# Split A-item epilogues and two-slot sigmoid buffers in an eight-core gated block

## What is computed

```python
xn = _layernorm(x, axis=-1)

# branch 1 (D_MODEL 2048, D_INNER 4096)
xn2 = (xn - mu) * rsqrt(var + 1e-5) * gamma + beta
z, gate = split(einsum('bsd,ed->bse', xn2, W_in), 2, axis=-1)
z_gated = z * sigmoid(clip(z, -15.0, 15.0))
z_temporal = z_gated * softmax(-dt)
b1 = einsum('bse,de->bsd', z_temporal * silu(clip(gate, -15.0, 15.0)), W_out) + xn

# branch 2 (H 2048, I 8192; weights are (int - 128) * scale)
g = einsum('bsh,ih->bsi', xn, Wg)
u = einsum('bsh,ih->bsi', xn, Wu)
b2 = einsum('bsi,hi->bsh', silu(g) * u, Wd)

return x + b1 + b2
```

## Time and profile before

| | us |
|---|---|
| median of 2 runs | 9599.44 (9590.61 to 9608.28) |
| profiled execution, its own time | 9556.24 |
| its span, slowest core (core 0) | 9554.7 |
| spans of the eight cores | 9482.8 to 9554.7 |
| TensorE busy, core 0 | 8093.0 |
| VectorE busy, core 0 | 3246.1 |
| ScalarE busy, core 0 | 755.3 |
| GpSimd busy, core 0 | 1138.1 |

### The profile page before, as it was taken

How to read it: one execution, slowest core, us unless ns; L and a number is a source line. 1 busy time by engine, 2 the same in 40 slices (tenths; PEclk the granted TensorE clock), 3 DMA queues, 4 the chain that set the end, 5 groups by cost and what they waited for, 6 DMA issues and landing times.

```text
span 9554.7 us, 87681 instructions; the slowest of 8 cores (9482.8 to 9554.7 us)
## 1 busy us (share of the span) xinstructions
PE 8093.0 (85%) x36127; PEld 3627.5 (38%) x36864; DVE 3246.1 (34%) x3151; ACT 755.3 (8%) x684; POOL 1138.1 (12%) x1093
## 2 busy tenths in 40 slices
PE   0006999999995899999996799999997788999998
PEld 0002444444442344444442344444443333444443
DVE  5542223333342232333333223233334232333334
ACT  3220000000000000000000000000000000000000
POOL 1000001111110010111110000111110101111110
PEclk9998999999997999999998899999998899999999
DMA  5554568777775567878776566777777566777777
GB/s 186 186 148 48 67 67 97 75 78 76 77 99 90 64 69 91 77 74 79 74 79 123 56 68 89 74 75 78 76 77 137 51 70 69 87 80 73 79 74 127
DMA packets 2296440, 827.99 MB, mean 87 GB/s; under 512 B 1997025, under 2 KB 2259185, under 8 KB 2287857
## 3 DMA queue, kind: packets, MB, share of 16 engines
q0 software_dynamic: 1857056, 570.53, 58.1%
q1 hardware_dynamic: 285394, 151.13, 6.4%
q10 hardware_dynamic: 153600, 100.69, 4.3%
HBM read 1241.64 MB, written 83.90 MB: 139 GB/s over the span
## 4 chain that ended last, share of the span: by engine, by line
PE 72%; DMA 13%; DVE 2%; issue 2%; another core or an unknown queue 1%; ACTq 1%; DVEq 1%; ACT 0%; POOL 0%; POOLq 0%
PE psZ L626 16%; PE psG L626 16%; DMA w1r<-w_inT 9%; PE psZ L571 9%; PE psOa L654 8%; PE psG L571 8%; PE psOb L654 8%; DMA wdr<-wdT 2%; PE psOa L571 1%; DMA xtck<-x_dt 1%; PE psOa L597 1%; PE psOb L597 1%; ACTq L733 1%; PE psOb L571 1%
## 5 line engine op out<-in xcount | busy, mean ns | idle before, releaser
L571 PE MATMUL psZ<-xnslot,w1r 128*128 128x512 bf16 x3513 | 880.5, 411 | 1160.7 <-DVE xnslot L810 805.3
L626 PE MATMUL psZ<-xnslot,gur 128*128 128x512 bf16 x7527 | 1691.9, 380 | 21.5 <-DVE gur L794 10.5
L626 PE MATMUL psG<-xnslot,gur 128*128 128x512 bf16 x7529 | 1687.5, 379 | 8.0
L794 DVE TENSOR_SCALAR gur<-gur 128x2048 bf16<-128x2048 bf16 x512 | 355.6, 696 | 2553.3 <-DMA gur<-wgT 1641.9
L626 PEld LDWEIGHTS psZ<-xnslot,gur 128*128 128x128 bf16 x7680 | 752.1, 98 | 924.7 <-issue 23.2
L626 PEld LDWEIGHTS psG<-xnslot,gur 128*128 128x128 bf16 x7680 | 751.4, 98 | 906.2
L571 PEld LDWEIGHTS psZ<-xnslot,w1r 128*128 128x128 bf16 x3584 | 365.6, 104 | 1674.9 <-issue 1337.0
L714 POOL DMA_DIRECT2D gur<-wgT x256 | 293.8, 1148 | 4527.5 <-PE psG L626 4198.3
L571 PE MATMUL psG<-xnslot,w1r 128*128 128x512 bf16 x3513 | 790.4, 380 | 3.8
L829 DVE TENSOR_SCALAR zcb<-psZ 128x1024 bf16<-128x1024 f32 x112 | 137.1, 1224 | 1770.8 <-PE psG L571 1706.9
L757 ACT ACTIVATE szcb<-psZ,sb_sg 128x1024 bf16<-128x1024 f32 x240 | 267.4, 1114 | 4826.0 <-PE psZ L626 4549.9
(11 more groups left out here) (86 smaller groups left out, 5435.1 us busy)
## 6 DMA issues: line engine op xcount, KB each, us to landing
w1r<-w_inT POOLq DMA_DIRECT2D x256, 512.0 KB, 9.6
gur<-wgT POOLq DMA_DIRECT2D x256, 512.0 KB, 8.7
gur<-wuT POOLq DMA_DIRECT2D x256, 512.0 KB, 12.2
wdr<-wdT POOLq DMA_DIRECT2D x256, 512.0 KB, 13.6
w2r<-wo_bf SPq DMA_DIRECT2D x256, 256.0 KB, 7.8
gx<-x_td SPq DMA_DIRECT2D x32, 1024.0 KB, 25.7
wo_in<-w_outT POOLq DMA_DIRECT2D x32, 1024.0 KB, 8.5
xtck<-x_dt ACTq DMA_DIRECT2D x64, 512.0 KB, 5.0
```

Of the source, the lines that this page charges most:

```text
L571: e.matmul(ps[:, th * TH:(th + 1) * TH], w1r[:, sl * 2048 + dc * 128: sl * 2048 + (dc + 1) * 128], xnslot[:, dc * TILE + th * TH: dc * TIL ...
L626: e.matmul(ps[:, th * TH:(th + 1) * TH], gur[:, sl * 2048 + dc * 128: sl * 2048 + (dc + 1) * 128], xnslot[:, dc * TILE + th * TH: dc * TIL ...
L794: M.do(lambda e, buf=buf: e.tensor_scalar_add(buf, buf, -128.0), c_dv, ("guc", t, c) if nn % 2 == 1 else None)
```

## The change

`zcb`, `gcb`, `szcb` and `sgcb` get two slots each; item i uses slot i mod 2 (C items: c mod 2, `szcb` only). On ScalarE, the sigmoid of C item c waits for `h` of c-2 instead of c-1.

On VectorE the work on an A item is cut into two functions. `ep_s1(i)` holds the wait for the item and the two clamps; `ep_s2(i)` waits for the sigmoids and does the three products (events `zg` and `act`). Up to i = 8 the list position of A item i holds `ep_s1(i)` and then `ep_s2(i-1)`; from i = 9 it holds `ep_s2(i-1)` and then `ep_s1(i)`; the position of item 31 ends with `ep_s2(31)`. The evictions of B items keep their places in the list. New waits of VectorE on its own events are added: `act` of i-1 in `ep_s2`, `h` of c-1 (or `act` of 31) before the first operation of a C item. The number of operations and of DMAs is the same, and TensorE's code and its waits are not changed.

```diff
@@ -494,10 +494,10 @@
             w2r = sst.enter_context(nc.sbuf_tensor("w2r", [128, R_W2 * 1024], BF16))
             gur = sst.enter_context(nc.sbuf_tensor("gur", [128, R_GU * 2048], BF16))
             wdr = sst.enter_context(nc.sbuf_tensor("wdr", [128, R_WD * 2048], BF16))
-            zcb = sst.enter_context(nc.sbuf_tensor("zcb", [128, TILE], BF16))
-            gcb = sst.enter_context(nc.sbuf_tensor("gcb", [128, TILE], BF16))
-            szcb = sst.enter_context(nc.sbuf_tensor("szcb", [128, TILE], BF16))
-            sgcb = sst.enter_context(nc.sbuf_tensor("sgcb", [128, TILE], BF16))
+            zcb = sst.enter_context(nc.sbuf_tensor("zcb", [128, 2 * TILE], BF16))
+            gcb = sst.enter_context(nc.sbuf_tensor("gcb", [128, 2 * TILE], BF16))
+            szcb = sst.enter_context(nc.sbuf_tensor("szcb", [128, 2 * TILE], BF16))
+            sgcb = sst.enter_context(nc.sbuf_tensor("sgcb", [128, 2 * TILE], BF16))
             p1b = sst.enter_context(nc.sbuf_tensor("p1b", [128, TILE], BF16))
             p2b = sst.enter_context(nc.sbuf_tensor("p2b", [128, TILE], BF16))
             xtck = sst.enter_context(nc.sbuf_tensor("xtck", [128, 2 * TILE], F32))
@@ -739,23 +739,27 @@
                 xp_half(M, d_xp, "X2", x2_scr, 0, range(16))
                 for t in range(nt):
                     for i in range(32):
+                        sl = (i % 2) * TILE
                         M.wait(c_dv, ("zc", t, i))
-                        M.do(lambda e: e.activation(szcb[:, :], zcb[:, :],
-                                                    AF.Sigmoid),
+                        M.do(lambda e, sl=sl: e.activation(
+                            szcb[:, sl:sl + TILE], zcb[:, sl:sl + TILE],
+                            AF.Sigmoid),
                              c_ac, ("szc", t, i))
                         M.wait(c_dv, ("gc", t, i))
-                        M.do(lambda e: e.activation(sgcb[:, :], gcb[:, :],
-                                                    AF.Sigmoid),
+                        M.do(lambda e, sl=sl: e.activation(
+                            sgcb[:, sl:sl + TILE], gcb[:, sl:sl + TILE],
+                            AF.Sigmoid),
                              c_ac, ("sgc", t, i))
                     M.wait(c_pe, ("A", t, 31))
                     xp_half(M, d_xp, "X1", xn_scr, t, range(16))
                     for c in range(64):
                         M.wait(c_pe, ("Cg", t, c))
-                        if c >= 1:
-                            M.wait(c_dv, ("h", t, c - 1))
+                        if c >= 2:
+                            M.wait(c_dv, ("h", t, c - 2))
                         pz, _ = zgp(c)
-                        M.do(lambda e, c=c, pz=pz: e.activation(
-                            szcb[:, :], pz[:, :], AF.Sigmoid,
+                        sl = (c % 2) * TILE
+                        M.do(lambda e, c=c, pz=pz, sl=sl: e.activation(
+                            szcb[:, sl:sl + TILE], pz[:, :], AF.Sigmoid,
                             scale=sb_sg[:, c:c + 1]),
                             c_ac, ("sg", t, c))
                     for dc in range(16):
@@ -816,36 +820,58 @@
 
                 affine(0)
                 for t in range(nt):
+                    def ep_s1(i):
+                        q = i // 8
+                        Q = 12 * t + q
+                        if i % 8 == 0 and Q >= 2:
+                            M.wait(c_pe, gen_consumer(Q - 2))
+                        M.wait(c_pe, ("A", t, i))
+                        pz, pg = zgp(i)
+                        sl = (i % 2) * TILE
+                        M.do(lambda e, pz=pz, sl=sl: e.tensor_scalar(
+                            zcb[:, sl:sl + TILE], pz[:, :], 15.0, -15.0,
+                            ALU.min, ALU.max), c_dv, ("zc", t, i))
+                        M.do(lambda e, pg=pg, sl=sl: e.tensor_scalar(
+                            gcb[:, sl:sl + TILE], pg[:, :], 15.0, -15.0,
+                            ALU.min, ALU.max), c_dv, ("gc", t, i))
+
+                    def ep_s2(i):
+                        q = i // 8
+                        pz, pg = zgp(i)
+                        sl = (i % 2) * TILE
+                        M.wait(c_ac, ("szc", t, i))
+                        M.wait(c_ac, ("sgc", t, i))
+                        if i >= 1:
+                            M.wait(c_dv, ("act", t, i - 1))
+                        elif t > 0:
+                            M.wait(c_dv, ("h", t - 1, 63))
+                        M.do(lambda e, pz=pz, sl=sl: e.tensor_mul(
+                            p1b[:, :], pz[:, :], szcb[:, sl:sl + TILE]),
+                            c_dv, ("zg", t, i))
+                        M.do(lambda e, sl=sl: e.tensor_mul(
+                            p2b[:, :], gcb[:, sl:sl + TILE],
+                            sgcb[:, sl:sl + TILE]))
+                        M.drain()
+                        ab = actA if q % 2 == 0 else actB
+                        s = i % 8
+                        M.do(lambda e, ab=ab, s=s: e.tensor_mul(
+                            ab[:, s * TILE:(s + 1) * TILE],
+                            p1b[:, :], p2b[:, :]),
+                            c_dv, ("act", t, i))
+
                     for it in items_by_tile[t]:
                         kind, _, idx = it
                         if kind == "A":
                             i = idx
-                            q = i // 8
-                            Q = 12 * t + q
-                            if i % 8 == 0 and Q >= 2:
-                                M.wait(c_pe, gen_consumer(Q - 2))
-                            M.wait(c_pe, ("A", t, i))
-                            pz, pg = zgp(i)
-                            M.do(lambda e, pz=pz: e.tensor_scalar(
-                                zcb[:, :], pz[:, :], 15.0, -15.0,
-                                ALU.min, ALU.max), c_dv, ("zc", t, i))
-                            M.do(lambda e, pg=pg: e.tensor_scalar(
-                                gcb[:, :], pg[:, :], 15.0, -15.0,
-                                ALU.min, ALU.max), c_dv, ("gc", t, i))
-                            M.wait(c_ac, ("szc", t, i))
-                            M.wait(c_ac, ("sgc", t, i))
-                            M.do(lambda e, pz=pz: e.tensor_mul(p1b[:, :], pz[:, :],
-                                                               szcb[:, :]),
-                                 c_dv, ("zg", t, i))
-                            M.do(lambda e: e.tensor_mul(p2b[:, :], gcb[:, :],
-                                                        sgcb[:, :]))
-                            M.drain()
-                            ab = actA if q % 2 == 0 else actB
-                            s = i % 8
-                            M.do(lambda e, ab=ab, s=s: e.tensor_mul(
-                                ab[:, s * TILE:(s + 1) * TILE],
-                                p1b[:, :], p2b[:, :]),
-                                c_dv, ("act", t, i))
+                            if i <= 8:
+                                ep_s1(i)
+                                if i >= 1:
+                                    ep_s2(i - 1)
+                            else:
+                                ep_s2(i - 1)
+                                ep_s1(i)
+                            if i == 31:
+                                ep_s2(31)
                         elif kind == "B":
                             j = idx
                             q, dc = j // 16, j % 16
@@ -871,10 +897,17 @@
                                 M.wait(c_pe, gen_consumer(Q - 2))
                             M.wait(c_ac, ("sg", t, c))
                             M.wait(c_pe, ("Cu", t, c))
+                            if c >= 1:
+                                M.wait(c_dv, ("h", t, c - 1))
+                            else:
+                                M.wait(c_dv, ("act", t, 31))
                             pz, pg = zgp(c)
-                            M.do(lambda e, c=c, pz=pz: e.scalar_tensor_tensor(
-                                p1b[:, :], pz[:, :], sb_sgu[:, c:c + 1],
-                                szcb[:, :], ALU.mult, ALU.mult))
+                            sl = (c % 2) * TILE
+                            M.do(lambda e, c=c, pz=pz, sl=sl:
+                                 e.scalar_tensor_tensor(
+                                     p1b[:, :], pz[:, :], sb_sgu[:, c:c + 1],
+                                     szcb[:, sl:sl + TILE],
+                                     ALU.mult, ALU.mult))
                             M.drain()
                             hb = actA if E % 2 == 0 else actB
                             s = c % 8
```

## The result

The ratio to the kernel before is **1.0069** (95% interval 1.0042 to 1.0097): 0.7% slower, or 66 us on 9599. The forecast was 1.2%, 111 us. The plain median of all 22 executions is 10315.05 us, beside 10062.84 us for the 19 of the kernel before; it lies outside the range of 9640 to 9790, and 9599.44 x 1.0069 = 9666 lies inside.

The account below looks back on a forecast made before the run. The prediction took the `w1r` panel loads to end TensorE's waits at A starts. Order 55, item 9 20, clock 27 and B 0 9 sum to 111 us; on 9599.44 that gives 9710 us, range 9640 to 9790.

Parts of the forecast that it names:

- What bounds the kernel: TensorE's A starts: the `w1r` weight panel ends the wait last, 472.7 us in 109 waits; `zg` has 3.7 us to spare.
- Slots, C items, self-waits, items up to 8: Double slots, looser ScalarE wait, VectorE self-waits and early A items: each claimed to cost or gain 0.
- The boundary at item 8: B item 0 starts 5.4 us later, waiting for item 7's `act`: 20 us at item 9, 9 us slow matmuls.
- The order from item 9 on: A items 10 to 31: product `p1b` falls behind an eviction, so starts come at +9.42 after `zcb`; 55 us lost.
- TensorE's clock: Starts after 2.6 us idle: 28 instead of 12 slow, 27 us more; bounds -20 and +99 us.
- the change would stay within 2%: Whole kernel: measured time within about 2% of the kernel before, chance 0.91; slower by over 2%, 0.08.
- a sum near 9660: Sign against the forecast, whole kernel: the low clock follows nearly none of the starts.
- (a): Rival at A starts: the panel still comes last; loss 29 us at most, 9600 to 9630; chance 0.12 with (d).
- (d): Rival at A starts: stage 2 is in time, only B 0 loses, about +29 us; chance 0.12 with (a).
- (b): Rival at TensorE restarts: every one at the low clock, 186 us, 9785, up to 277; chance beyond 190 us 0.07.
- (c): Rival on ScalarE: its sigmoid round trip was on TensorE's path; 161.8 us saved, 9438, 1.7% less; chance 0.03.

Follow-up runs that it names:

- Four slots: The kernel before with four slots instead of three in the weight-panel ring `w1r`; 8923 us against 9572.
- the two kernels of one chip: Kernel before with only the changed VectorE order from item 9 on (9616 us), and kernel before with only the two slots and new waits (9571 us).
- one short operation more: Kernel with only the late order from item 9 on, `p2b` now made ahead of product `p1b`; 9769 us, 153 above that kernel.
- the product twice: Kernel with only the late order from item 9 on, product `p1b` made twice, only the second signalling `zg`; 9884 us, 268 above that kernel.
- four-slot changed kernel: The changed kernel with four slots instead of three in `w1r`, products written in place; 9432 us, 509 above the kernel before with four slots.
- three-matmul kernel: The four-slot changed kernel with three further matmuls at the head of each A item from 9 on; 9459 us on one die.

## Why the prediction was off in size

**What bounds the kernel.** Right: the panel ended the waits. Four slots took out 467 of 471 us on core 5.

**Slots, C items, self-waits, items up to 8: 0.** Right, 9571 against 9572 for the first three; the skewed early items still wait for the panel (284.1 us from `zcb` to start after, 285.0 before, in 32 starts).

**The boundary at item 8: 20 + 9 us.** Right: +5.1 for B 0, and 30 us in all at item 9. In these 30 the slow matmuls of B 0 are 6.5, where 9 were forecast.

**The order from item 9 on: 55 us.** Right: 52 us between the traces before and after, and 43 us between the two kernels of one chip. Every time of the chain (+6.90, +8.04, +9.4, idle 2.6) is in the profile within 0.02 us.

**TensorE's clock: 27 us. This is the step that failed.** Measured: -4. The step took the share of slow starts from the neighbouring groups of starts in the kernel before (16 of 40), and predicted 16 more slow starts. There were 3 more (26.2 against 23.2 of 88), with less extra time than before, and on one chip 2 fewer (28.0 against 30.0). The share that was carried over had been read rightly: over all eight cores before, 91 of 236 starts after 1.9 to 2.6 us were slow. After the change it was 79 of 307 at 2.6 to 2.7 us, and one slow start cost 1.46 us instead of 1.68. The groups before had mixed distances from start to start. After the change nearly all fast starts are 23.5 us apart, and there one start in four is slow; with three matmuls more, 0.65 us, it was one in seven, with six one in two. So the share before could not be carried over, and this trace had no row from which the new one could have been read. Why a distance has the share it has stays open. The bounds of the step (-20 to +99) did hold it.

Of the 39 us between the forecast of 111 and the 72 in the traces, the clock makes 31, items up to 8 make 6, and the order and the boundary 2. 55 + 20 + 9 = 84 us would have been the sum without this step, 0.9%, against a measured 66 us (40 to 93). The direction was right, and so was that the change would stay within 2%. The prediction named a sum near 9660 as a sign that almost no start would be slow; 9666 came with a quarter of them slow, because as many had been slow before.

**The rivals.** (a) and (d) are excluded by the 88 waits for `p1b`. (b), every restart at the low clock, did not happen at 2.6 us, but nearly did at 3.2 us, in the experiment with one short operation more (631 of 660). The Trainium skill (TensorE: Matmul & The Clock Gate, Part 1) says that the low level is the array's default, which activity lifts, and counts its cost at each restart. The trace agrees at 3.2 us of idle time, and at 2.6 us in one start of four. 0.6 us of idle time more per start cost 153 us. The mean surcharge of the 88 starts there was 1.6 us, short of the 1.8 that the forecast named for passing 2%, but with the added pauses that kernel was 193 us above before, which is 2.0%. The start of 10.03 us that (b) takes from the earlier trace rows does not show a low level beyond the first 32 matmuls, as (b) reads it: the 10.03 us are those of the 32. (c) is excluded by the four-slot kernel of before: VectorE still waits 1.25 us for the second sigmoid there, and no start waits for the product.

## What to carry to other kernels

When a list of work is skewed by one item, ask for each event of the delayed half who waits for it on another engine, and what stands between its old place and its new one. Here the product that frees the accumulator moved behind an eviction that waits for TensorE. If a long wait hides the error, measure it with that wait removed: 66 us became 509 us. And the wait that did the hiding was worth more than the reordering: one more slot in the ring of weight panels saved 6.8%.

## What the runs showed of the hardware

Equal pauses of TensorE do not cost equally. After 2.61 us of idle time one start in four, one in seven or one in two was slow, at 23.5, 24.1 and 24.8 us from one fast start to the next, in regular patterns. After 3.21 us or more (one short operation more) it was 631 of 660, and after 3.91 us or more (the product twice) 432 of 440, with 9.6 us for the 32 matmuls instead of 7.07. In the kernel before, over eight cores, none of 336 starts after less than 1.9 us was slow, and 60 of 64 beyond 3.4 us were.

In a slow start only a part of the 32 matmuls runs at the low level of the clock (1.2 instead of 2.4 GHz), and it needn't be the first ones. In the four-slot changed kernel the start at 1184.24 found a granted clock of 0.50, and its first matmuls are 0.43 us apart instead of 0.22. In the three-matmul kernel the start at 1207.24 began at a granted clock of 1.00 (1207.3 to 1208.4), and 0.50 came behind it (1208.6 to 1211.8). What comes after a pause can so be slowed down when it has already begun.

Removing the pauses altogether took more than their sum off: on core 5 485 us of pauses in the A stage, and 610 us of its time.
